# Loading the staged feed-forward weights (sequences 17 to 22) from ScalarE's DMA queue instead of the sync engine's

## The chip, the cores and the metric

The kernel runs on one core of one Trainium2 chip. The metric is the device time of one execution in microseconds; the time of a kernel is the median of several executions. Profiles come from one profiled execution each. TensorE (PE) does matmuls and transposes, VectorE (DVE), ScalarE (ACT) and GpSimd (POOL) do elementwise work, and the sync engine (SP) only issues DMAs. ScalarE can issue DMAs too, through a queue of its own; such an issue stands in its instruction stream between its activations.

## The reference

One transformer block on 16 sequences of 256 rows and 256 features, all in float32: self-attention, cross-attention to a context of 192 features, and a gated feed-forward layer.

```
h = _layernorm(x, ln1_g, ln1_b)
x = _attention(h, h, sa_wq, sa_wk, sa_wv, sa_wo, sa_bo) + x
h = _layernorm(x, ln2_g, ln2_b)
x = _attention(h, cond_emb, ca_wq, ca_wk, ca_wv, ca_wo, ca_bo) + x
h = _layernorm(x, ln3_g, ln3_b)
p = h @ ff_w1 + ff_b1
a, gate = (p[..., :D_FF], p[..., D_FF:])
h = a * jax.nn.gelu(gate, approximate=False) @ ff_w2 + ff_b2
return h + x
```

Attention has 16 heads of 64 features. ff_w1 is 256 x 2048, ff_w2 is 1024 x 256.

## The kernel before, in words

Each matmul operand is split into a rounded high part and a low remainder, and products are made of three passes (high by high, high by low, low by high), so that the result keeps float32 accuracy.

The attention work is cut into 256 slots `c`, one for each pair of heads of each sequence: `seq, pair = divmod(c, PAIRS)` with PAIRS = 8. Sequences 0 to 15 are the self-attention, 16 to 31 the cross-attention of the same 16 inputs. The feed-forward layer runs after slot 255. Each engine runs its own loop over the slots, and semaphores tie the loops together: `pe_slot`, `act_slot`, `dve_slot`, `pool_slot`, and for the sync engine the loop over `c` in its block. All of it is software-pipelined by hand, in written order.

What happens to one pair of heads `k`: TensorE projects its queries and keys into the PSUM bank QKB three slots early (`pe_project`, L342). ScalarE copies QKB, rounded, into QKS (`act_copy_qk`, L470), VectorE writes the low part into QKS (`dve_split_qk`, L604) and so frees QKB for the next projection. The sync engine then copies QKS into RX in four DMAs (`copy_ring`, L434 and L436). TensorE reads RX for the scores S (L303, L304). QKS has two buffers, so ScalarE's copy of `k` waits for the RX copies of `k - 2` to have landed. The scores pass a maximum on VectorE (L616), the exponential on ScalarE (L508, PT), transposes on TensorE (L356, PTB), a rounding copy on ScalarE (L529, PH) with its low part on VectorE (L598, PL), the product with the values (L401, PVB), a copy of half of it on ScalarE (L485, ON), the division by the denominators on POOL (L814), and the output projection (L381, WOP).

In every slot the sync engine issues seven DMAs: two that spread denominators (`spread_den`, L1241), one that saves them (`save_den`, L1230) and the four of `copy_ring`. At pair 0 `store_rows` adds one (L1213), and after that `weights(c)` may add some. ScalarE's queue carries the loads of turned rows (`act_load_rows`, L442, two of its four before the exponentials of pair 1 and two at the end of that slot) and of the context (`act_load_ctx`, L460).

STG is one buffer of 128 partitions by 1024 columns for weights on their way from DRAM. The weights of the cross-attention pass through it in sequences 1 to 6, its output weights after those, and those of the feed-forward layer in sequences 17 to 22: at pair 0 the sync engine waits until POOL has read the previous contents and issues two DMAs of 64 partitions, 256 KB each (L1201). POOL then splits a quarter at each of the pairs 2, 5, 6 and 7 (`pool_split_w`, L756 and L758, into WA), and counts each in `s_pw`. Sequences 17 to 20 bring ff_w1 (rows of 4 KB), 21 and 22 bring ff_w2 (rows of 1 KB).

Of the kernel before, what the change touches and what calls it, by code (L numbers as in the profile page):

```python
# [11 lines left out]
P = 128  # L12
B, S, D = 16, 256, 256
# [6 lines left out]
PAIRS = H // 2  # L20
# [5 lines left out]
CH = 1024  # L26
HC = CH // 2
NCH = 6
HALF = PAIRS // 2
HOLD = 8  # L30
QTR = 4
# [46 lines left out]
def block_kernel(nc, x, ctxt, ln1_g, ln1_b, ln2_g, ln2_b, ln3_g, ln3_b, sa_wq, sa_wk, sa_wv, sa_wo,  # L78
                 sa_bo, ca_wq, ca_wk, ca_wv, ca_wo, ca_bo, ff_w1, ff_b1, ff_w2, ff_b2, out):
    ctx = ExitStack()  # L80
    with ctx:
        def sb(name, shape, dt=F32):
            return ctx.enter_context(nc.sbuf_tensor(name, shape, dt))
# [4 lines left out]
        def sem(name):  # L88
            return ctx.enter_context(nc.semaphore(name))
# [19 lines left out]
        STG = sb("STG", [P, CH])  # L109
# [47 lines left out]
        def await_low(e, n):  # L157

            if n in DVE_LOW:
                e.wait_ge(s_wlo, DVE_LOW.index(n) + 1)  # L160
            else:
                e.wait_ge(s_wlp, POOL_LOW.index(n) + 1)
# [11 lines left out]
        d_wst = sem("d_wst")  # L174
# [15 lines left out]
        s_pw = sem("s_pw")  # L190
        s_oh = sem("s_oh")
        s_ow = sem("s_ow")
# [228 lines left out]
        def act_gain_bias(e, n, k):  # L421

            e.wait_ge(a.dve_th, n)
            h = near(n)[:, k * S:(k + 1) * S]
            e.activation(h, h, ACT.Identity, bias=LNG[:, n // B, 1, k:k + 1],
                         scale=LNG[:, n // B, 0, k:k + 1]).then_inc(a.act_hf, 1)
# [18 lines left out]
        def act_load_rows(e, n, *parts):  # L445

            e.wait_ge(d_hs, 16 * n)
            e.wait_ge(a.s_ht, 2 * n)
            if n >= B:
                e.wait_ge(a.pl_ct, 2 * (n - B + 1))  # L450
            load_turned(e, far(n), HS[0, :, :], d_hl, *parts)
# [21 lines left out]
        def act_slot(e, sl):  # L473
            c = sl.c
            seq, pair = divmod(c, PAIRS)
            prepares = c >= 0 and sl.has(PAIRS * (seq + 1))

            if sl.has(c - 3):
                s = c - 3
                sl.wait(e, a.pe_pv, s + 1)  # L480
                sl.wait(e, a.pl_o, s - 1)
                if s == 0:
                    e.wait_ge(s_ow, HALF)
                for i in range(2):
                    last = e.activation(ON[OWN[i], s % 2, :], PVB[OTHER[i], i * S:(i + 1) * S], ACT.Copy)  # L485
                last.then_inc(a.act_lp, 1)

            if prepares:
                if pair == 1 and seq:
                    act_load_rows(e, seq + 1, 0, 1)  # L490
                if pair in (3, 4):
                    act_gain_bias(e, seq + 1, pair - 3)
            if pair in (3, 4, 5) and sl.has(PAIRS * (seq + 2)) and seq + 2 >= B:
                act_load_ctx(e, seq + 2, *((0,), (3,), (6, 7))[pair - 3])

            if 0 < c < DIRECT:
                act_copy_qk(e, c + 2)

            if sl.has(c):
                sl.wait(e, a.pe_t, c - 1)  # L500
                sl.wait(e, a.dve_rc, c - 1)
                if c == 1:
                    await_low(e, 2)
                for i in range(2):
                    sl.wait(e, a.dve_nm, 2 * c + i + 1)
                    for qt in range(TT):
                        j = i * TT + qt
                        last = e.activation(PT[:, c % 2, j * S:(j + 1) * S], S1[:, i, qt * S:(qt + 1) * S],  # L508
                                            ACT.Exp, bias=NM[:, j:j + 1], accum_out=DEN[:, c % 2, j:j + 1])
                    last.then_inc(a.act_exp, 1)  # L510

            if c == 0:
                act_copy_qk(e, 2)
            elif sl.has(c + AHEAD) and not -1 <= c < DIRECT - 1:
                act_copy_qk(e, c + AHEAD)

            if ATT - 8 <= c < ATT - 6:
                load_ffn_rows(e, 0, 4 * (c - ATT + 8) + 1, 4 * (c - ATT + 8) + 3)

            if c == ATT:  # L520
                e.wait_ge(a.pe_t, ATT - 1)
                e.activation(FG[:, 1, 0:1], B1[:, PAIRS:PAIRS + 1], ACT.Gelu).then_inc(s_tab, 1)
                act_ffn(e, Slot(0, FU, 2))

            if sl.has(c - 1):
                s = c - 1
                sl.wait(e, a.pe_t, s + 1)
                sl.wait(e, a.pe_pv, s - 1)
                e.activation(PH[:, s % 2, :], PTB[:, :, :].rearrange("p i n -> p (i n)"), ACT.Copy) \  # L529
                    .then_inc(a.act_ph, 1)  # L530

            if c in (ATT - 4, ATT - 3):
                act_ffn_h(e, 0, c - ATT + 4)

            if prepares and pair == 1:
                act_load_rows(e, seq + 1, *(range(2, 4) if seq else range(4)))
            if pair in (3, 4) and sl.has(PAIRS * (seq + 2)) and seq + 2 >= B:
                act_load_ctx(e, seq + 2, *((1, 2), (4, 5))[pair - 3])
# [562 lines left out]
        def dve_weights(e, *ns):  # L1101

            for n in ns:
# [6 lines left out]
                else:  # L1110
                    e.tensor_tensor(low, raw(n), hi, ALU.subtract).then_inc(s_wlo, 1)

        def act_attention_slot(e, sl):
            act_slot(e, sl)
            if -AHEAD <= sl.c < 3:
                act_weights(e, *((4,), (5,), (6, 7), (8,), (9, 10), (11,))[sl.c + AHEAD])
            if sl.c == PAIRS * 2:
                e.wait_ge(d_sm, 16 * 5)
# [53 lines left out]
        def _(e):  # L1172
# [24 lines left out]
            def stage(src, dst=STG[:, :]):  # L1197

                h = P // 2
                for part, rows in ((slice(0, h), src[0]), (slice(h, P), src[1])):  # L1200
                    e.dma_start(dst[part], rows).then_inc(d_wst, 16)  # L1201

            def stage_rows(w):

                v = w.rearrange("(g p) n -> p g n", p=P)
                stage((v[0:P // 2], v[P // 2:P]), STG[:, :].rearrange("p (g n) -> p g n", n=D))
# [16 lines left out]
            half = DA // 2  # L1223
# [28 lines left out]
                else:  # L1252
                    stage((w[P:DC, :], w[P:DC, :]))

            def stage_ffn(n):

                if n < 4:
                    w = ff_w1[n // 2 * P:(n // 2 + 1) * P, n % 2 * CH:(n % 2 + 1) * CH]
                    stage((w[0:P // 2, :], w[P // 2:P, :]))
                else:  # L1260
                    stage_rows(ff_w2[(n - 4) * half:(n - 3) * half, :])

            def spill(c):

                seq, pair = divmod(c, PAIRS)
# [11 lines left out]
            def weights(c):  # L1277

                seq, pair = divmod(c, PAIRS)
                if c == 1:  # L1280
                    e.dma_start(BOUT[:, :], sa_bo.partition_broadcast(P)).then_inc(d_bo, 16)
                if 2 <= c < HOLD:
                    await_low(e, c + 4)
                    load_x(xv, c)
                if c == 3:
                    await_low(e, 4)
                    await_low(e, 5)
                    stage_rows(sa_wo[half:, :])
                if c == PAIRS + 2:
                    load_gains(1, ln2_g, ln2_b)  # L1290
                if c == PAIRS + 3:
                    load_gains(2, ln3_g, ln3_b)
                if c == PAIRS + 4:
                    e.dma_start(B1[:, :], ff_b1.rearrange("(k p) -> p k", p=P),
                                allow_slow_non_contiguous=True).then_inc(d_sm, 16)
                if pair == 0 and 1 <= seq <= NCH:
                    if seq == 1:
                        e.wait_ge(s_ow, PAIRS)
                    else:
                        e.wait_ge(s_pw, QTR * (seq - 1))  # L1300
                    stage_cross(seq - 1)
                if c == PAIRS * (NCH + 1) + 1:
                    e.wait_ge(s_pw, QTR * NCH)
                    stage_rows(ca_wo[0:half, :])
                if c == SLOTS - PAIRS - 1:
                    e.wait_ge(a.pl_xb, B)
                    e.dma_start(BOUT[:, :], ca_bo.partition_broadcast(P)).then_inc(d_bo, 16)
                if c == SLOTS + 1:
                    e.wait_ge(s_ow, PAIRS + HALF)
                    stage_rows(ca_wo[half:, :])  # L1310
                if pair == 0 and B + 1 <= seq <= B + NCH:
                    if seq == B + 1:
                        e.wait_ge(s_ow, 2 * PAIRS)
                    else:
                        e.wait_ge(s_pw, QTR * (NCH + seq - B - 1))
                    stage_ffn(seq - B - 1)
                if c == ATT - PAIRS:
                    e.wait_ge(a.pl_xb, 2 * B)
                    e.dma_start(BOUT[:, :], ff_b2.partition_broadcast(P)).then_inc(d_bo, 16)
# [136 lines left out]
```

## Time and profile before

| | |
|---|---|
| median of 3 runs | 1713.91 us |
| lowest to highest | 1712.26 to 1714.52 us |
| profiled execution, its time | 1712.7 us |
| profiled execution, span of the trace | 1710.7 us |
| TensorE busy | 1699.1 us, 99% of the span |
| VectorE busy | 1468.2 us, 86% |
| ScalarE busy | 1186.5 us, 69% |
| GpSimd busy | 1087.7 us, 64% |
| granted TensorE clock | 1.000 |

Issues of DMAs are not counted as busy time. The shares are averages over the whole span, of which the attention slots take the first four fifths. Names such as SPq and ACTq stand for an engine's DMA issues; the duration beside one is that of the issue, not of the transfer.

### The profile page before, as it was taken

To read this page: it belongs to the slowest core of one execution; us is meant where nothing else is said; L and a number is where in the kernel's file an instruction comes from. 1 tells how busy PE (TensorE), PEld (TensorE's weight loads), DVE (VectorE), ACT (ScalarE), POOL (GpSimd) and SP (SyncE) were. 2 spreads that over 40 slices of the span, in tenths; PEclk is the share of its full clock that TensorE was granted. 3 is DMA by queue.
4 is the path that set the end of the run, shared out by engine and by line. 5 is a ranking of instruction groups with operands and counts; after the bars stand their busy time and mean duration, and the time that the engine had idled before them with its cause. 6 is when DMAs were issued, how large, how long until landed. Compare 5 with 4: busy or idle time off the path is not lost.

```text
span 1710.7 us, 42980 instructions
## 1 busy us (share of the span) xinstructions
PE 1699.1 (99%) x13628; PEld 1661.8 (97%) x13628; DVE 1468.2 (86%) x3184; ACT 1186.5 (69%) x3246; POOL 1087.7 (64%) x1812
## 2 busy tenths in 40 slices
PE   8999999999999999999999999999999999999999
PEld 8999999999999999999999999999999998888888
DVE  8888988888888888899999999999999998666665
ACT  7777777777777777777777777887787776222222
POOL 6777777766666666687777887777777666122211
PEclk9999999999999999999999999999999999999999
DMA  7777777676666566667777787776666663212110
GB/s 210 186 187 177 185 182 180 167 181 165 154 156 155 150 161 160 166 166 185 191 189 194 188 194 180 182 181 168 169 170 168 164 167 80 68 50 68 64 42 25
DMA packets 286640, 263.99 MB, mean 154 GB/s; under 512 B 102224, under 2 KB 246736, under 8 KB 286416
## 3 DMA queue, kind: packets, MB, share of 16 engines
q1 hardware_dynamic: 232624, 248.12, 57.2%
q10 hardware_dynamic: 53792, 13.12, 3.7%
q8 instruction: 111, 1.82, 0.4%
q14 instruction: 113, 0.93, 0.2%
HBM read 70.40 MB, written 24.90 MB: 56 GB/s over the span
## 4 chain that ended last, share of the span: by engine, by line
PE 94%; SPq 1%; POOL 1%; DMA 1%; DVE 1%; issue 1%; ACT 1%; ACTq 0%; POOLq 0%; DVEq 0%
PE QKB L342 19%; PE PVB L401 14%; PE PTB L356 12%; PE WOP L381 10%; PE VB L317 9%; PE S L304 7%; PE S L303 7%; PE PTB L923 5%; PE S L923 5%; PE QKB L939 3%; PE VB L939 3%; SPq L434 0%; SPq L436 0%; ACT PT L508 0%; DMA STG<-in_L_xattn_ca_wo_dram 0%
## 5 line engine op out<-in xcount | busy, mean ns | idle before, releaser
L508 ACT ACTIVATE PT<-S,NM 128x256 f32<-128x256 f32 x1024 | 472.1, 474 | 183.9 <-DVE NM L616 183.4
L598 DVE TENSOR_TENSOR PL<-PTB,PH 128x512 fp32r<-128x512 f32 x512 | 349.6, 684 | 80.1 <-ACT PH L529 76.1
L814 POOL TENSOR_TENSOR ON<-ON,RB 128x256 f32<-128x256 f32 x256 | 188.8, 738 | 275.0 <-DVE ON L636 261.6
L616 DVE TENSOR_REDUCE NM<-S 128x2 f32<-128x512 f32 x512 | 326.1, 678 | 0.0
L529 ACT ACTIVATE PH<-PTB 128x1024 fp32r<-128x1024 f32 x256 | 263.5, 1029 | 88.9 <-PE PTB L356 85.8
L356 PE MATMUL PTB<-IDN,PT 128*128 128x128 f32 x2048 | 265.9, 273 | 0.1
L303 PE MATMUL S<-RX 128*128 128x256 f32 x1012 | 253.8, 283 | 0.0
L304 PE MATMUL S<-RX 128*128 128x256 f32 x1012 | 253.7, 283 | 0.0
L356 PEld LDWEIGHTS PTB<-IDN,PT 128*128 128x128 f32 x2048 | 229.5, 140 | 0.9 <-DVE PL L598 0.8
L381 PE MATMUL WOP<-WO,OT 128*128 128x256 f32 x1536 | 226.3, 283 | 1.7 <-POOL OT L819 1.7
L636 DVE TENSOR_TENSOR ON<-PVB,ON 64x256 f32<-64x256 f32 x512 | 213.3, 417 | 3.5
L508 ACT ACTIVATION_READ_ACCUMULATOR PT<-S,NM 128x1 f32 x1024 | 207.9, 203 | 0.0
L485 ACT ACTIVATE ON<-PVB 64x256 f32<-64x256 f32 x512 | 194.3, 379 | 17.4 <-issue 3.0
L381 PEld LDWEIGHTS WOP<-WO,OT 128*128 128x128 f32 x1536 | 202.7, 192 | 2.3 <-POOL OT L819 2.1
L342 PE MATMUL QKB<-HT,WA 128*128 128x256 f32 x1512 | 202.4, 283 | 2.3 <-DVE QKS L604 1.3
L819 POOL TENSOR_TENSOR OT<-ON,OT 128x256 fp32r<-128x256 f32 x256 | 189.7, 741 | 20.5
L795 POOL TENSOR_TENSOR VR<-VF,VR 128x256 fp32r<-128x256 f32 x256 | 189.7, 741 | 20.5
L304 PEld LDWEIGHTS S<-RX 128*128 128x128 f32 x1012 | 194.3, 192 | 0.0
L342 PEld LDWEIGHTS QKB<-HT,WA 128*128 128x128 f32 x1512 | 190.4, 192 | 3.2 <-issue 2.3
L303 PEld LDWEIGHTS S<-RX 128*128 128x128 f32 x1012 | 193.4, 191 | 0.0
L401 PE MATMUL PVB<-PH,VR 128*128 128x256 f32 x1024 | 183.5, 300 | 1.6 <-issue 1.5
L604 DVE TENSOR_TENSOR QKS<-QKB,QKS 128x512 fp32r<-128x512 f32 x254 | 166.0, 654 | 17.0 <-ACT QKS L470 16.9
(143 smaller groups left out, 3140.0 us busy)
## 6 DMA issues: line engine op xcount, KB each, us to landing
RX<-QKS SPq DMA_DIRECT2D x506, 192.0 KB, 2.9
RX<-QKS SPq DMA_DIRECT2D x506, 128.0 KB, 2.8
RB<-denominators SPq DMA_DIRECT2D x512, 64.0 KB, 2.7
out_dram<-XR SPq DMA_DIRECT2D x32, 256.0 KB, 2.7
rows<-XN SPq DMA_DIRECT2D x24, 256.0 KB, 2.4
rows<-HF SPq DMA_DIRECT2D x23, 256.0 KB, 2.6
XR<-in_x_dram SPq DMA_DIRECT2D x16, 256.0 KB, 3.2
denominators<-RDT SPq DMA_DIRECT2D x256, 16.0 KB
```

The lines of the kernel that those rows point to most:

```text
L303: e.matmul(o, q, RX[:, c % 2, i, K1, :], start=True, stop=False)
L304: last = e.matmul(o, q, RX[:, c % 2, i, K2, :], start=False, stop=True)
L342: last = e.matmul(qk_bank(k)[:, m * S:(m + 1) * S], w[:, p * P:(p + 1) * P], act, start=j == 0, stop=j == len(passes) - 1)
L356: last = e.transpose(PTB[:, i, kt * S + qt * P:kt * S + (qt + 1) * P], PT[:, s % 2, q0:q0 + P], IDN[:, :])
L381: last = e.matmul(WOP[:, t * D:(t + 1) * D], OT[:, op, t * P:(t + 1) * P], WO[:, p, wp, :], start=p == 0 and t == 0 and j == 0, stop=p == ...
L401: last = e.matmul(PVB[:, i * S:(i + 1) * S], VR[:, s // 2 % 2, kt, s % 2, i * P:(i + 1) * P], part[:, first:first + S], start=i == 0 and j ...
L485: last = e.activation(ON[OWN[i], s % 2, :], PVB[OTHER[i], i * S:(i + 1) * S], ACT.Copy)
L508: last = e.activation(PT[:, c % 2, j * S:(j + 1) * S], S1[:, i, qt * S:(qt + 1) * S], ACT.Exp, bias=NM[:, j:j + 1], accum_out=DEN[:, c % 2 ...
L529: e.activation(PH[:, s % 2, :], PTB[:, :, :].rearrange("p i n -> p (i n)"), ACT.Copy) \
L598: e.tensor_tensor(PL[:, cols], PTB[:, i, :], PH[:, s % 2, cols].bitcast(F32), ALU.subtract).then_inc(a.dve_pl, 1)
L616: e.tensor_reduce(NM[:, i * TT:(i + 1) * TT], S1[:, i, :].rearrange("p (t s) -> p t s", t=TT), AX.X, ALU.max, negate=True).then_inc(a.dve_ ...
L636: last = e.tensor_tensor(on, PVB[OWN[i], i * S:(i + 1) * S], on, ALU.add)
```

## The change

`stage_ffn` moves from the sync engine's `weights(c)` to `act_attention_slot`. ScalarE now makes the same waits and issues the same twelve DMAs, two at the end of its slot at pair 0 of sequences 17 to 22, behind its PH copy. The destinations, sizes and the semaphore `d_wst`, for which POOL waits, stay.

```diff
         def act_attention_slot(e, sl):
             act_slot(e, sl)
+            seq, pair = divmod(sl.c, PAIRS)
+            if pair == 0 and B + 1 <= seq <= B + NCH:
+                if seq == B + 1:
+                    e.wait_ge(s_ow, 2 * PAIRS)
+                else:
+                    e.wait_ge(s_pw, QTR * (NCH + seq - B - 1))
+                stage_ffn(e, seq - B - 1)
...
+        def stage_ffn(e, n):
+
+            h = P // 2
+            if n < 4:
+                w = ff_w1[n // 2 * P:(n // 2 + 1) * P, n % 2 * CH:(n % 2 + 1) * CH]
+                for rows in (slice(0, h), slice(h, P)):
+                    e.dma_start(STG[rows, :], w[rows, :]).then_inc(d_wst, 16)
+            else:
+                w = ff_w2[(n - 4) * HC:(n - 3) * HC, :].rearrange("(g p) n -> p g n", p=P)
+                to = STG[:, :].rearrange("p (g n) -> p g n", n=D)
+                for rows in (slice(0, h), slice(h, P)):
+                    e.dma_start(to[rows], w[rows]).then_inc(d_wst, 16)
...
-                if pair == 0 and B + 1 <= seq <= B + NCH:
-                    if seq == B + 1:
-                        e.wait_ge(s_ow, 2 * PAIRS)
-                    else:
-                        e.wait_ge(s_pw, QTR * (NCH + seq - B - 1))
-                    stage_ffn(seq - B - 1)
```

ScalarE's stream before, from the end of slot 144 (pair 0 of sequence 18) into slot 145; PT is the exponential, QKS the copy of the projections, PH the rounded transposes, ON the copy of the attention product, HF<-rows the first two row loads of pair 1:

```order
L470 ACTIVATE QKS<-QKB 128x512 [waits d_dup1,pe_qk]
L529 ACTIVATE PH<-PTB 128x1024 [waits pe_pv,pe_t]
L485 ACTIVATE ON<-PVB 64x256 [waits pl_o,pe_pv]
L485 ACTIVATE ON<-PVB 64x256
L442 DMA HF<-rows 32x4x128 [waits pl_ct,s_ht,d_hs]
L442 DMA HF<-rows 32x4x128
L508 ACTIVATE PT,DEN<-S,NM 128x256 [waits dve_nm,dve_rc,pe_t]
```

The same place in the changed kernel:

```order
L470 ACTIVATE QKS<-QKB 128x512 [waits d_dup1,pe_qk]
L529 ACTIVATE PH<-PTB 128x1024 [waits pe_pv,pe_t]
L1119 DMA STG<-in_L_xattn_ff_w_dram 64x1024 [waits s_pw]
L1119 DMA STG<-in_L_xattn_ff_w_dram 64x1024
L485 ACTIVATE ON<-PVB 64x256 [waits pl_o,pe_pv]
L485 ACTIVATE ON<-PVB 64x256
L442 DMA HF<-rows 32x4x128 [waits pl_ct,s_ht,d_hs]
L442 DMA HF<-rows 32x4x128
L508 ACTIVATE PT,DEN<-S,NM 128x256 [waits dve_nm,dve_rc,pe_t]
```

Two DMA issues with a wait for POOL now stand between PH and ON, ahead of the row loads in the same queue.

The sync engine's stream before, at pair 0 of sequence 17 (slot 136) and into slot 137; RX<-QKS are the four ring copies, RB<-denominators and denominators<-RDT the denominators:

```order
L1230 DMA denominators<-RDT 4x32x32 [waits d_rb1,dve_rt]
L434 DMA RX<-QKS 64x768 [waits pe_s,dve_lo]
L436 DMA RX<-QKS 64x2x256
L434 DMA RX<-QKS 64x768
L436 DMA RX<-QKS 64x2x256
L1201 DMA STG<-in_L_xattn_ff_w_dram 64x1024 [waits s_ow]
L1201 DMA STG<-in_L_xattn_ff_w_dram 64x1024
L1241 DMA RB<-denominators 64x256 [waits pl_or,d_ds3]
L1241 DMA RB<-denominators 64x256
L1230 DMA denominators<-RDT 4x32x32 [waits d_rb0,dve_rt]
L434 DMA RX<-QKS 64x768 [waits pe_s,dve_lo]
```

The same place in the changed kernel (L1250 and L1261 are the former L1230 and L1241):

```order
L1250 DMA denominators<-RDT 4x32x32 [waits d_rb1,dve_rt]
L434 DMA RX<-QKS 64x768 [waits pe_s,dve_lo]
L436 DMA RX<-QKS 64x2x256
L434 DMA RX<-QKS 64x768
L436 DMA RX<-QKS 64x2x256
L1261 DMA RB<-denominators 64x256 [waits pl_or,d_ds3]
L1261 DMA RB<-denominators 64x256
L1250 DMA denominators<-RDT 4x32x32 [waits d_rb0,dve_rt]
L434 DMA RX<-QKS 64x768 [waits pe_s,dve_lo]
```

The two loads of STG are gone from between the ring copies of one slot and the denominators of the next; nothing else moved on this engine.

## Rows read from the trace of the kernel before

**Rows 1.** The page: busy time, share of the span, instructions.
```profile
PE 1699.1 (99%) x13628; PEld 1661.8 (97%) x13628; DVE 1468.2 (86%) x3184; ACT 1186.5 (69%) x3246; POOL 1087.7 (64%) x1812
```

**Rows 2.** Timeline, TensorE (start, duration): projections, slot 136, 137, then sequences' starts.
```profile
783.10 0.76 PE L342 MATMUL QKB<-CT,WB 128*128 128x256 f32 x5
...
788.91 0.76 PE L342 MATMUL QKB<-CT,WB 128*128 128x256 f32 x5
...
826.89 0.76 PE L342 MATMUL QKB<-CT,WB 128*128 128x256 f32 x5
...
870.89 0.76 PE L342 MATMUL QKB<-CT,WB 128*128 128x256 f32 x5
...
914.91 0.76 PE L342 MATMUL QKB<-CT,WB 128*128 128x256 f32 x5
...
958.72 0.76 PE L342 MATMUL QKB<-CT,WB 128*128 128x256 f32 x5
...
1002.08 0.76 PE L342 MATMUL QKB<-CT,WB 128*128 128x256 f32 x5
...
1045.64 0.76 PE L342 MATMUL QKB<-CT,WB 128*128 128x256 f32 x5
...
1089.00 0.76 PE L342 MATMUL QKB<-CT,WB 128*128 128x256 f32 x5
```

**Rows 3.** Timeline, TensorE: the projections of slots 154 to 156 (sequence 19).
```profile
881.73 0.82 PE L342 MATMUL QKB<-CT,WB 128*128 128x256 f32 x5
...
887.45 0.86 PE L342 MATMUL QKB<-CT,WB 128*128 128x256 f32 x5
...
893.24 0.76 PE L342 MATMUL QKB<-CT,WB 128*128 128x256 f32 x5
```

**Rows 4.** Timeline, ScalarE and its queue, 873 to 887 us.
```profile
874.61 1.02 ACT L529 ACTIVATE PH<-PTB 128x1024 fp32r<-128x1024 f32 x1
...
875.66 0.38 ACT L485 ACTIVATE ON<-PVB 64x256 f32<-64x256 f32 x1
876.04 1.33 ACTq L442 DMA_DIRECT2D XN<-rows  x1
...
877.49 0.48 ACT L508 ACTIVATE PT<-S,NM 128x256 f32<-128x256 f32 x1 [1.07 <-DVE NM L616]
...
880.31 0.60 ACT L470 ACTIVATE QKS<-QKB 128x512 fp32r<-128x512 f32 x1 [0.88 <-DMA RX<-QKS]
...
886.07 0.60 ACT L470 ACTIVATE QKS<-QKB 128x512 fp32r<-128x512 f32 x1 [0.87 <-DMA RX<-QKS]
```

**Rows 5.** Timeline, the sync engine's issues, same stretch.
```profile
875.49 0.62 SPq L436 DMA_DIRECT2D RX<-QKS  x1
876.14 1.87 SPq L1201 DMA_DIRECT2D STG<-in_L_xattn_ff_w_dram  x2
878.12 1.18 SPq L1241 DMA_DIRECT2D RB<-denominators  x2
...
880.09 0.49 SPq L434 DMA_DIRECT2D RX<-QKS  x1
...
881.96 0.62 SPq L436 DMA_DIRECT2D RX<-QKS  x1
```

**Rows 6.** Timeline, VectorE: the low part of QKS for pair 155.
```profile
874.82 0.65 DVE L604 TENSOR_TENSOR QKS<-QKB,QKS 128x512 fp32r<-128x512 f32 x1
```

**Rows 7.** Timeline, POOL: the last quarter read from STG before slot 152.
```profile
869.18 0.75 POOL L758 TENSOR_TENSOR WA<-STG,WA 128x256 fp32r<-128x256 f32 x1
```

**Rows 8.** The DMAs issued from 780 to 1010 us: KB each, median us to landing.
```profile
RX<-QKS SPq DMA_DIRECT2D x83, 192.0 KB, 2.9
...
STG<-in_L_xattn_ff_w_dram SPq DMA_DIRECT2D x12, 256.0 KB, 4.9
```

**Rows 9.** Waits of ScalarE from 780 to 1010 us: total, times, longest.
```profile
ACT QKS L470 <- DMA RX<-QKS: 7.7, 8, 1.4
```

**Rows 10.** Window of sequence 23: length, busy PE, PEld, DVE, ACT, POOL, clock, DMA, GB/s.
```profile
1045.64:1089.00 43.36, 43.36 (x370) 43.36 (x369) 40.73 (x90) 34.71 (x99) 32.10 (x56) 1.00 0.75 187
```

More of the change, by code:

```diff
@@ L1253, in stage_cross @@
                     stage((w[P:DC, :], w[P:DC, :]))
[L1255 to L1259, printed above, removed]
-                else:
-                    stage_rows(ff_w2[(n - 4) * half:(n - 3) * half, :])
             def spill(c):
@@ L1310, in weights @@
                     stage_rows(ca_wo[half:, :])
-                if pair == 0 and B + 1 <= seq <= B + NCH:
-                    if seq == B + 1:
-                        e.wait_ge(s_ow, 2 * PAIRS)
-                    else:
-                        e.wait_ge(s_pw, QTR * (NCH + seq - B - 1))
-                    stage_ffn(seq - B - 1)
                 if c == ATT - PAIRS:
```

## The prediction

> **What bounds the kernel now.** I read the page first, then TensorE's timeline slot by slot, then the same stretch on the other engines. TensorE is busy for 1699.1 of 1710.7 us [rows 1], so all its gaps together are 11.6 us, and no change of queues can bring more. What the moved loads can have to do with any of it is read from the starts of TensorE's projections at pair 0 [rows 2]. Sequence 23, without staging, takes 1089.00 - 1045.64 = 43.36 us, or 5.42 a slot. The six sequences with staging take 43.79, 44.00, 44.02, 43.81, 43.36 and 43.56, which is 0.43, 0.64, 0.66, 0.45, 0.00 and 0.20 more: 2.38 us together. Of the first 0.43, 0.39 belongs to slot 136 itself (788.91 - 783.10 = 5.81), before a byte of ff_w1 has been asked for. So about 2.0 us of the span stand beside the staging at all, nearly all of it in sequences 18 to 20.
>
> How the 0.66 of sequence 19 comes about is in its rows. In slot 154 and 155 TensorE loses 5.72 - 5.42 = 0.30 and 5.79 - 5.42 = 0.37 [rows 3]. ScalarE's copy of QKS began at 880.31 and again at 886.07, both after waiting some 0.9 us for an RX copy to land [rows 4], and a late QKS makes the VectorE split late, which frees QKB for the next projection. The second of these waits is for the ring copies issued from 880.09 to 882.58. Their source was ready at 874.82 + 0.65 = 875.47 [rows 6], so they went out 4.6 us late, because the sync engine issues in order and was busy: the two loads of STG took it 1.87 us, then denominators, then the copies [rows 5]. VectorE has no room to catch up: it is busy for 40.73 of 43.36 us even without staging [rows 10]. ScalarE met such a wait 8 times in this stretch, 7.7 us in all, the longest 1.4 [rows 9].
>
> **The change, part by part.** *Removed from the sync engine:* two issues a sequence. In sequence 19 the sync engine was free at 875.49 + 0.62 = 876.11 and began the denominators of the next slot at 878.12 [rows 5]; without the loads that is 2.0 us sooner, and so are the copies behind them: 878.1 to 880.6 in place of 880.09 to 882.58. The last is issued at 879.95 in place of 881.96; with the 2.9 us from issue to landing [rows 8] it lands near 882.9, and even with the 4.1 that it took here (881.96 to 886.07) at 884.1, 2.0 us ahead of 886.07, so the second wait goes. The first (880.31) is for ring copies issued before the loads and is not helped by this. Sequence 21 shows no loss at all with the same staging on the same queue [rows 2], so a staging as such need not cost anything; I take it that the losses of 18, 19, 20 and 22 go with the second wait: 0.64 + 0.66 + 0.45 + 0.20 = 1.95 us. The lower bound is nothing, if another late thing stands right behind.
>
> *Added to ScalarE:* twelve issues. An issue does not occupy its arithmetic, but what is behind it in the stream waits. Nothing shows this DMA on ACTq, so I bound it: the pair is 1.87 us here on the sync engine as the dear end [rows 5], and 0.6 each, 1.2 us, by the ring copy's row (875.49, 0.62) of the same order of size as the cheap end. The issues can begin when PH has been handed to the engine at 874.61 [rows 4], so they end between 875.8 and 876.5, where ON now starts at 875.66; ON moves by 0.2 to 0.8 us. The two row loads of pair 1 come next; the second took 1.33 us beside the two STG issues of the sync engine, and it is its end (877.37) that let the exponentials go at 877.49 [rows 4]. With the sync engine's STG issues gone it should be nearer to the ring copy's 0.6. So the exponentials of slot 153 start between 877.1 and 878.3, against 877.49 now: 0.4 sooner to 0.8 later. Behind them stands the QKS copy, which waits until 880.31 anyway: the exponentials now end at about 879.4, 0.9 before it, which covers the 0.8. If the cover were gone, TensorE would lose about what it lost in slot 154, 0.30. I take half of that, 0.15 for each of six sequences, 0.9 us.
>
> The new wait costs nothing: POOL finished the last quarter at 869.18 + 0.75 = 869.93 [rows 7], 4.7 us before ScalarE comes to it. POOL's own need is distant: it reads STG two slots later, and the landing of 4.9 us [rows 8] starts about 1.5 us earlier than now. ScalarE's row loads now stand behind 512 KB in their queue, but only the last two of the four, a slot later, decide when the rows are there.
>
> *The transfers themselves:* same bytes. They begin at about 874.7 in place of 876.14, from another queue than the ring copies of the same slot (873.6 to 876.1). This is what speaks against the change. Where rows show it: the ring copies of that slot, issued before the loads, landed just ahead of 880.31, 4.8 us after the last of them was issued at 875.49, where the median is 2.9 [rows 4, 5, 8]; the loads disturb even copies that were issued before them, by 1.9 us. 512 KB at the 187 GB/s of this stretch [rows 10] is 2.8 us of the engines' time. From below the added delay is nothing (they are disturbed already), from above the whole 2.8 us, if all of the loads is served ahead of them. I take a value near nothing, because the loads will be 1.4 us further on when the last ring copy is issued.
>
> The Trainium skill, page "DMA: Bandwidth & Descriptors", sections "Queues, rings and completion order" and "Issuing engines are not separate DMA queues", says that each DMA engine takes turns between the queues that have work, a packet at a time, and that issuing from several engines only saves the sequencer's issue time. By that rule the ring copies lose the place ahead of the loads that they have in one queue, and what is saved is the sync engine's 1.87 us alone; it makes the rival of the shared turns below more likely than the rows alone would, and leaves the sum as it is.
>
> Sum: -1.95 + 0.9 = -1.05 us. The profiled execution was 1712.7 us, a span of 1710.7 and 2.0 around it; it would be 1711.65, with a span of 1709.65. The median of the runs is 1713.91, 1.2 above the profiled one, so I predict 1712.9. A measurement of this kernel can tell about 0.2%, 3.4 us, from no change; the runs before spread over 2.3 us.
>
> **The rivals.**
> *Nothing moves* (25%). The second wait goes, but the losses have another cause, such as VectorE's row turn in the same slot, or ScalarE gives all of it back. For it: sequence 17 loses 0.39 in slot 136 with no staging near it [rows 2], so such losses have other sources. Time 1713.9, plus or minus 0.4.
> *All is won* (12%). ScalarE's issues are wholly hidden: -1.95, a time of 1712.0.
> *The ring copies of the same slot give way to the loads* (15%), the case on the other side. The loads take their turns on the DMA engines between ring copies that until now were ahead of them. The first wait grows by up to 2.8 us; QKS, split and projection follow, as VectorE has no room. It decides once the landing is late by more than about 0.3 us beyond now, since at 880.31 the split only just meets the projection at 881.73 [rows 3]. Price: at half of it, 1.4 - 0.3 = 1.1 us in each of six sequences, 6.6, less the 1.95 won: +4.65, 1718.6; at a quarter, 0.7 - 0.3 = 0.4 each, 2.4 less 1.95, +0.45, 1714.4. Against it: the copies have 1.4 us less of loads ahead of their end than behind them now.
> *ScalarE's issues get long* (8%). If each of the two takes the 1.33 of the row load that was issued beside others [rows 4], the pair ends at 877.3, the row loads 1.7 us later, and exponentials start at 879.0, 1.5 late; 0.9 is covered, 0.6 is not: 3.6 over six, less 1.95, +1.6, 1715.6.
>
> The Trainium skill, page "Perfetto Trace Analysis", section "DMA Instruction — HWDGE (DVE, Sync)", says that the two issuing engines share one descriptor generator, and that the profiled time of an issue holds the wait for its lock. The 1.33 us row load beside the 1.87 us pair agrees with it [rows 4, 5].
>
> **How the numbers follow.** The forecast (1712.4 to 1713.4 by its own terms) has 40%, the rivals 25, 12, 15 and 8. The gain cannot pass 2.4 us, and a change of over 3.4 us down needs something outside this stretch: faster 0.03. Over 3.4 us up needs the half of the ring rival's chance that lies at such delays: 0.08. Same: 0.89. The range goes from 1711.2 (all is won, and the spread of a median of three) to 1715.8 (the cheap part of the ring rival, and the long issues).
>
> **What would show it.** In the changed profile: sequences 18 to 20 at 43.4 to 43.6 us between projections, against 44.0; no wait of QKS for RX in slot 154, 162 and so on, one left in the slot before; ring copies at pair 1 issued some 2 us sooner; the STG issues on ACTq at 0.6 to 0.95 us each, beginning within PH; the exponentials of the next slot within 0.8 us of the 5.42 us beat. I would be wrong if the wait of pair 1's QKS copy grows beyond 1.4 us, or if these sequences get longer than 44.0.

## The result and the profile after

The changed kernel takes 1717.08 us (median of 17 executions) against 1713.32 for the kernel before (17 executions), a ratio of 1.0022 with a 95% interval of 1.0016 to 1.0029. It is slower by 3.8 us. Predicted were 1712.9 us, a small gain, with a range of 1711.2 to 1715.8. One of these executions took 4702.53 us, and one of e3_sp_early below 2049.97; both were disturbed, and the ratios leave them out. The profiled execution took 1719.83 us, one of the longer ones, with a span of 1717.9; what its profile loses is therefore more than the 3.8 us between the medians.

The page of the changed kernel, its busy times and the chain that ended last:

```profile
PE 1700.6 (99%) x13628; PEld 1662.6 (97%) x13628; DVE 1467.7 (85%) x3184; ACT 1185.0 (69%) x3246; POOL 1085.2 (63%) x1812
...
PE 87%; POOL 3%; SPq 2%; DMA 2%; ACT 2%; DVE 2%; issue 2%; POOLq 0%; ACTq 0%; DVEq 0%
```

The instructions are as many as in [rows 1]. Only TensorE is busy longer, by 1.5 us (its weight loads by 0.8), and the span is 7.2 us longer: the other 5.7 us are waiting. Where it is can be read from windows that end at TensorE's projection at pair 0 of each sequence, here sequences 18 to 23 (length, busy PE, PEld, DVE, ACT, POOL, granted clock, DMA, GB/s):

```profile
826.93:872.48 45.55, 43.89 (x370) 43.48 (x369) 40.66 (x90) 34.55 (x99) 34.60 (x61) 1.00 0.76 183
872.48:917.64 45.16, 43.85 (x370) 43.44 (x369) 40.63 (x90) 34.53 (x99) 34.57 (x61) 1.00 0.77 185
917.64:961.00 43.36, 43.36 (x370) 43.36 (x369) 40.75 (x90) 34.67 (x99) 34.79 (x61) 1.00 0.80 192
961.00:1008.20 47.20, 45.27 (x370) 44.86 (x369) 40.76 (x90) 34.66 (x99) 34.77 (x61) 0.96 0.75 177
1008.20:1052.64 44.44, 44.05 (x370) 43.50 (x369) 40.56 (x90) 34.48 (x99) 34.53 (x61) 1.00 0.78 187
1052.64:1096.00 43.36, 43.36 (x370) 43.36 (x369) 40.71 (x90) 34.65 (x99) 31.97 (x56) 1.00 0.76 188
```

Sequence 23, without staging, takes 43.36 us as before. In excess of that, sequences 18, 19, 21 and 22 take 2.19, 1.80, 3.84 and 1.08 us; sequence 20 takes none, and sequence 17 (783.02 to 826.93, not shown) 0.55. The six make 9.46 us, against 2.38 before [rows 2]. That difference, 7.1 us, is the whole difference of the two spans.

The waits of the changed kernel from 780 to 1045 us say what for (total, times, longest):

```profile
ACT QKS L470 <- DMA RX<-QKS: 10.0, 5, 3.5
PEld S L303 <- DMA RX<-QKS: 5.3, 4, 1.9
PE S L303 <- DMA RX<-QKS: 4.5, 4, 1.7
```

TensorE now waits for RX itself, four times; in the whole profile before it never did. Sequence 18 shows how. ScalarE and its queue at the end of slot 144 and in slot 145:

```profile
830.65 1.03 ACT L529 ACTIVATE PH<-PTB 128x1024 fp32r<-128x1024 f32 x1
830.65 1.15 ACTq L1119 DMA_DIRECT2D STG<-in_L_xattn_ff_w_dram  x2
831.91 0.38 ACT L485 ACTIVATE ON<-PVB 64x256 f32<-64x256 f32 x1 [0.23 <-issue]
832.04 1.37 ACTq L442 DMA_DIRECT2D HF<-rows  x1
...
834.20 0.48 ACT L508 ACTIVATE PT<-S,NM 128x256 f32<-128x256 f32 x1 [1.52 <-DVE NM L616]
...
838.49 0.60 ACT L470 ACTIVATE QKS<-QKB 128x512 fp32r<-128x512 f32 x1 [2.35 <-DMA RX<-QKS]
```

The two loads of STG are issued beside the PH copy, and hold ON up by 0.23 us. The next exponentials start 7.27 us behind the projection of pair 0, against 6.33 before, but it is the QKS copy that stands still, for 2.35 us, until the ring copies of slot 144 have landed. The same landing, at 838.45, is what TensorE's scores wait for; when they are done, the next projection still waits 0.20 us for the split of that late QKS copy:

```profile
838.45 0.39 PE L303 MATMUL S<-RX 128*128 128x256 f32 x1 [1.47 <-DMA RX<-QKS]
...
839.86 0.86 PE L342 MATMUL QKB<-CT,WB 128*128 128x256 f32 x5 [0.20 <-DVE QKS L604]
```

These are the sync engine's issues at the same time:

```profile
829.23 0.75 SPq L434 DMA_DIRECT2D RX<-QKS  x1
830.03 0.62 SPq L436 DMA_DIRECT2D RX<-QKS  x1
830.71 0.60 SPq L434 DMA_DIRECT2D RX<-QKS  x1
831.35 2.07 SPq L436 DMA_DIRECT2D RX<-QKS  x1
833.52 1.19 SPq L1261 DMA_DIRECT2D RB<-denominators  x2
```

The loads of STG (830.65 to 831.80) fall between the second and the fourth ring copy. The two L436 copies of this slot, minimum, median and maximum from issue to landing:

```profile
DMA to landing us min/median/max: 4.6/5.8/7.1
```

In the kernel before, the same two of sequence 18 took

```profile
DMA to landing us min/median/max: 3.5/4.2/5.0
```

and in sequence 21, before, 2.8 to 3.1. The last ring copy takes 2.1 us longer to land than before, and 3.2 us longer in sequence 21, where it is 6.3 in place of 3.1. Two other things add to the lateness. In sequence 18 the issue of that copy alone took 2.07 us in place of 0.62, beside a row load on ScalarE's queue (832.04); it isn't needed for the damage, since in sequence 19 this issue took 0.62 us and the copy still landed after 6.6 us in place of 4.7. In sequence 21 the ring copies were issued 1.0 us later than before, behind a row store (L1233, the former L1213) whose issue took 1.63 us in place of 0.53.

What TensorE loses follows from the point at which the last ring copy of pair 0 lands. In sequences 18 to 22 of the changed kernel that is 11.5, 11.1, 8.6, 11.7 and 10.2 us behind the projection of pair 0, and the slot of pair 1 takes 2.08, 1.72, 0.00, 2.36 and 0.81 us more than 5.42: each about the time by which the landing passes 9.4 us. Before, it landed at 9.6, 9.3, 8.9, 7.5 and 7.7 us, and the slot of pair 1 lost 0.19 us in sequence 18 and nothing in the others. So the copies of sequences 18 and 19 had no slack left before the change.

In sequence 21 something is added. After the stall, TensorE's granted clock fell (changed kernel, windows of 2 us):

```profile
970.00:972.00 2.00, 1.04 (x9) 0.84 (x8) 0.00 (x0) 0.00 (x0) 1.77 (x4) 1.00 1.13 211
972.00:974.00 2.00, 1.22 (x8) 1.02 (x8) 0.55 (x1) 1.18 (x2) 1.45 (x3) 0.98 1.12 255
974.00:976.00 2.00, 1.80 (x8) 1.80 (x9) 1.78 (x4) 1.32 (x4) 0.00 (x0) 0.50 1.09 218
976.00:978.00 2.00, 2.00 (x14) 2.00 (x13) 1.82 (x5) 2.00 (x9) 0.31 (x1) 0.67 0.78 172
978.00:980.00 2.00, 2.00 (x19) 2.00 (x19) 1.79 (x5) 0.82 (x2) 1.76 (x4) 1.00 0.78 199
```

TensorE was half idle for four microseconds, then ran at 0.50 of full speed, the 1.2 GHz level, for 2 us and was back at 2.4 GHz within the next two. The slot after the stall took 6.88 us between projections in place of 5.42, so the clock took up to 1.5 us of this profile. The 2 us windows around the stall in sequence 18 (834 to 844 us) all have clock 1.00; sequence 21 has the longer of the two stalls.

### The profile page after: what moved, and what is told of

Its sections match the earlier page's. It is cut to its first block, busy times and chain, and to the rows that moved or that the text cites. A ratio compares the mean times of both kernels' runs of the same rounds, so it can differ in the third digit from the quotient of the medians.

```text
span 1717.9 us, 42980 instructions
## 1 busy us (share of the span) xinstructions
PE 1700.6 (99%) x13628; PEld 1662.6 (97%) x13628; DVE 1467.7 (85%) x3184; ACT 1185.0 (69%) x3246; POOL 1085.2 (63%) x1812
## 4 chain that ended last, share of the span: by engine, by line
PE 87%; POOL 3%; SPq 2%; DMA 2%; ACT 2%; DVE 2%; issue 2%; POOLq 0%; ACTq 0%; DVEq 0%
PE QKB L342 18%; PE PVB L401 12%; PE PTB L356 11%; PE WOP L381 9%; PE VB L317 8%; PE S L304 6%; PE S L303 6%; PE PTB L923 5%; PE S L923 5%; PE QKB L939 3%; PE VB L939 3%; DMA RX<-QKS 1%; ACT PT L508 1%; SPq L434 1%; ACT PH L529 1%
```

## The experiments

Three theories. BYTES: the 512 KB of a staging share the DMA engines with the ring copies of pair 0, which are short of time, and now start among them rather than behind them. STREAM: the two issues hold up ScalarE's own work. QUEUE: a second queue by itself, taking turns with the sync engine's, delays the ring copies, whenever the loads start. The kernel before was measured beside each of them; its median was 1713.48 us beside e1 to e4, 1713.88 beside e5 to e8 and 1713.42 beside e9 to e11.

### e1_act_tiny: the changed kernel with a quarter of each load

```diff
-                    e.dma_start(STG[rows, :], w[rows, :]).then_inc(d_wst, 16)
+                    e.dma_start(STG[rows, 0:QW], w[rows, 0:QW]).then_inc(d_wst, 16)
...
-                    e.dma_start(to[rows], w[rows]).then_inc(d_wst, 16)
+                    e.dma_start(to[rows, 0:1], w[rows, 0:1]).then_inc(d_wst, 16)
```

> The twelve loads stay where the change put them on ScalarE, but bring a quarter of the columns (64 KB each in place of 256 KB), so that the feed-forward weights and the output are not the real ones. Theory BYTES (the loads now start about 1.5 us sooner, among the ring copies of the same slot, and share the DMA engines with them): the ring copies land in time, the waits of TensorE for RX are gone, and the kernel is 1 to 2 us below the kernel before (about 1712). Theory STREAM (the two issues hold up ScalarE's exponentials and copies): the issues are as many and as long, so the time stays near that of the changed kernel, 3 to 4 us above the kernel before.

Measured: 1711.81 us, ratio 0.9992 (0.9983 to 1.0001), 1.7 us below the kernel before, as BYTES has it. Sequences 18 to 21 in its windows:

```profile
828.94:872.30 43.36, 43.36 (x371) 43.36 (x369) 40.63 (x90) 34.53 (x99) 34.65 (x61) 1.00 0.74 183
872.30:915.66 43.36, 43.36 (x371) 43.36 (x369) 40.62 (x90) 34.67 (x99) 34.71 (x61) 1.00 0.75 183
915.66:959.02 43.36, 43.36 (x371) 43.36 (x369) 40.74 (x90) 34.65 (x99) 34.79 (x61) 1.00 0.73 183
959.02:1002.38 43.36, 43.36 (x371) 43.36 (x369) 40.63 (x90) 34.70 (x99) 34.79 (x61) 1.00 0.74 183
```

TensorE never waits in them, with all twelve issues in ScalarE's stream. In one place the issues were even long, and the exponentials waited for them (ScalarE, sequence 18):

```profile
832.66 2.41 ACTq L1119 DMA_DIRECT2D STG<-in_L_xattn_ff_w_dram  x2
835.16 0.38 ACT L485 ACTIVATE ON<-PVB 64x256 f32<-64x256 f32 x1 [1.48 <-POOL OT L819]
...
836.31 0.47 ACT L508 ACTIVATE PT<-S,NM 128x256 f32<-128x256 f32 x1 [0.38 <-issue]
```

and that sequence is 43.36 us long like the others. STREAM falls as the cause of the changed kernel's loss. (For ff_w1 the quarter is rows of 1 KB in place of 4, of the same number. Whether what counts is the bytes or the length of the rows this run doesn't separate; e6_act_split below moves whole rows away instead.)

### e2_sp_tiny: the kernel before with a quarter of each load

```diff
-                    stage((w[0:P // 2, :], w[P // 2:P, :]))
+                    stage((w[0:P // 2, 0:QW], w[P // 2:P, 0:QW]), STG[:, 0:QW])
...
-                    stage_rows(ff_w2[(n - 4) * half:(n - 3) * half, :])
+                    w = ff_w2[(n - 4) * half:(n - 3) * half, :].rearrange("(g p) n -> p g n", p=P)
+                    stage((w[0:P // 2, 0], w[P // 2:P, 0]), STG[:, 0:QW])
```

> The loads are on the sync engine as before, a quarter of the columns each, so the output is not the real one. It shows what the bytes of the staging cost in the kernel before. BYTES: 1 to 2 us below the kernel before, near e1_act_tiny. If the sync engine's lateness by the issues were what costs the kernel before its 2 us, as the prediction had it, the time stays at the kernel before and e1_act_tiny is faster than this by 1 to 2 us. STREAM says that e1_act_tiny is slower than this by 3 to 5 us.

Measured: 1711.98 us, ratio 0.9991 (0.9982 to 1.0000), the same as e1_act_tiny. So the bytes of the staging cost the kernel before most of its 2 us, and the sync engine's issues little. The profiles leave the issues something: the six sequences exceed 43.36 by 1.22 us here and by 0.58 in e1_act_tiny, 0.39 and 0.40 of these in sequence 17. The times don't resolve that 0.6. ScalarE still waits for RX 8 times here, 4.9 us in all from 780 to 1045 us, and never in e1_act_tiny: the issues do make ring copies late, and TensorE feels little of it.

### e3_sp_early and e11_sp_early_look: the sync engine's queue, right ahead of the ring copies

```diff
+                seq, pair = divmod(c, PAIRS)
+                if pair == 0 and B + 1 <= seq <= B + NCH:
...
+                    stage_ffn(seq - B - 1)
                 if 0 <= c - 1 + AHEAD < ATT and c - 1 >= -AHEAD:
                     k = c - 1 + AHEAD
```

(The same lines are taken out of `weights(c)`, as in e10_sp_first. e11_sp_early_look is the same kernel again, with a profile to read.)

> The full loads on the sync engine's queue, ahead of the four ring copies of the same slot in place of behind them. BYTES, in the form that the start ahead of the ring copies is what counts, whichever the queue: ring copies land 2 us or more later than before, TensorE waits for RX in most of the six sequences, 4 to 12 us above the kernel before. Theory QUEUE (a second queue taking turns is what delays the ring copies, not when the loads start): only the 1.3 us of later issue counts, 0 to 2 us above the kernel before.

> The kernel of e3_sp_early once more, for its profile. BYTES: TensorE waits for RX in most of the sequences 17 to 22, and the last of the four ring copies of pair 0 takes 5 to 7 us from issue to landing, against 3.1 to 5.0 in the kernel before.

Measured: 1721.16 us, ratio 1.0040 (1.0027 to 1.0054), and 1722.28 for the single execution of e11_sp_early_look. With one queue only, the loss is twice that of the changed kernel. The waits of e11_sp_early_look from 780 to 1045 us:

```profile
ACT QKS L470 <- DMA RX<-QKS: 15.2, 6, 3.6
PEld S L303 <- DMA RX<-QKS: 6.1, 5, 1.8
PE S L303 <- DMA RX<-QKS: 5.0, 4, 1.6
```

In its sequence 19 the L436 copies took 4.6 to 5.4 us to land, and they were issued 1.1 to 1.2 us later than before as well. Of the 1.9 us by which the last one landed later, 1.2 are the later issue and 0.7 the transfer, so this run alone doesn't separate the two; e10_sp_first does. The loss of 7.7 us is far above the 0 to 2 that QUEUE allowed, so a second queue is not needed for the damage: QUEUE falls as the cause, BYTES stands.

### e4_act_pair1: ScalarE's queue, behind the first row loads of pair 1

```diff
                     act_load_rows(e, seq + 1, 0, 1)
+                if pair == 1 and B + 1 <= seq <= B + NCH:
...
+                    stage_ffn(e, seq - B - 1)
```

(In e4, e5 and e7 the lines of the change are taken out of `act_attention_slot`.)

> The full loads on ScalarE's queue, but behind the first two row loads of pair 1, about 2 us later than in the changed kernel and near the time at which the sync engine issued them. BYTES: within 1 us of the kernel before, or up to 1.5 us faster since the sync engine is free. QUEUE: still 3 to 4 us slower, since the queue is the second one. STREAM: 3 us or more slower, since the exponentials of pair 1 now stand right behind the issues.

Measured: 1714.16 us, ratio 1.0003 (0.9994 to 1.0012). On the second queue, but near the old time, the loads cost what they cost before. TensorE never waited for RX. This is the other half of the answer on QUEUE. The gain from a freed sync engine did not show either. On STREAM the answer is less clean: the issues stood right ahead of the exponentials, and in sequence 20, where the row loads ahead of them were late too, these waited 3 us:

```profile
923.96 0.47 ACT L514 ACTIVATE PT<-S,NM 128x256 f32<-128x256 f32 x1 [2.99 <-issue]
```

That sequence took 1.88 us more than 43.36, with its last ring copy landed 7.5 us behind the projection, in good time. So in this place ScalarE's stream can cost TensorE something; the median doesn't resolve it. POOL waited 5 times for STG, 6.4 us in all, which TensorE's waits don't show.

### e5_act_on: ScalarE's queue, 4.5 us earlier than the change put them

```diff
                 last.then_inc(a.act_lp, 1)

+            if pair == 0 and B + 1 <= seq <= B + NCH:
...
+                stage_ffn(e, seq - B - 1)
```

> The full loads on ScalarE's queue at the same pair 0, but ahead of the exponentials, 4 us earlier than in the changed kernel, so that the 2.8 us of transfer are mostly over when the sync engine issues the ring copies of this slot. BYTES, if what counts is the overlap with those four ring copies and their small slack: the waits of TensorE for RX are gone, and the kernel is 0.5 to 2 us below the kernel before. If what counts is any start ahead of the ring copies (as a simple reading of e3_sp_early has it): 4 us or more above. The ring copies of the slot before have about 1 us more slack and take the disturbance.

Measured: 1712.71 us against 1713.88, ratio 0.9990 (0.9981 to 0.9998): faster than both kernels, if only just. The loads, on ScalarE's queue, and the ring copies of the same slot, on the sync engine's, in sequence 19:

```profile
871.59 0.48 ACTq L1125 DMA_DIRECT2D STG<-in_L_xattn_ff_w_dram  x1
...
872.11 0.62 ACTq L1125 DMA_DIRECT2D STG<-in_L_xattn_ff_w_dram  x1
```

```profile
875.00 0.63 SPq L434 DMA_DIRECT2D RX<-QKS  x1
...
876.99 0.62 SPq L436 DMA_DIRECT2D RX<-QKS  x1
```

The L436 copies land in 3.3 to 4.0 us, and what is left of ScalarE's waits for RX from 780 to 1045 us is

```profile
ACT QKS L470 <- DMA RX<-QKS: 0.7, 2, 0.4
```

against 8.7 us before in the same stretch and 10.0 after the change. Sequences 18 to 20 take 43.36 us each. So it is not any start ahead of the ring copies that hurts; 3.4 us ahead is harmless, and 0.3 to 1.4 us behind the first of them is the bad place (in sequence 20 not even that).

### e6_act_split: one load at pair 0, one at pair 1

```diff
-                stage_ffn(e, seq - B - 1)
+                stage_ffn(e, seq - B - 1, slice(0, P // 2))
...
                     act_load_rows(e, seq + 1, 0, 1)
+                    if B + 1 <= seq <= B + NCH:
+                        stage_ffn(e, seq - B - 1, slice(P // 2, P))
```

> The first load stays where the change put it, the second goes behind the first two row loads of pair 1. BYTES: half of the burst among the ring copies, so their landing is late by about half (1 us in place of 2 to 3.5), which the slack nearly covers: 0 to 1.5 us above the kernel before. A theory by which the mere order of issue counts: 3 us above.

Measured: 1714.43 us against 1713.88, ratio 1.0000 (0.9992 to 1.0009). Half of the burst in the bad place costs nothing that can be told by the time. In its profile TensorE waited twice for RX, 1.5 us, against four times and 4.5 us in the changed kernel, and the slots of pair 1 lost 1.26 us in sequence 18 and 1.44 in sequence 20, whose last ring copies landed at 10.6 and 10.8 us.

### e7_act_pair1_exp: ScalarE's queue, behind the exponentials of pair 1

```diff
+            if pair == 1 and B + 1 <= seq <= B + NCH:
...
+                stage_ffn(e, seq - B - 1)
             if c == 0:
                 act_copy_qk(e, 2)
```

> The full loads on ScalarE's queue behind the exponentials of pair 1, 4 to 5 us later than in the changed kernel. BYTES: the ring copies of pair 0 are out of reach, those of pair 1 share with the loads, in the slot where the sync engine is not held up by a row store: 0.5 us above to 1.5 us below the kernel before, if POOL, which wants STG at pair 2, is not kept waiting for more than 2 us. If POOL's wait for STG decides, POOL's waits for this DMA appear in its list and it is 1 to 4 us above.

Measured: 1717.45 us against 1713.88, ratio 1.0016 (1.0007 to 1.0025). Its waits from 780 to 1045 us have both:

```profile
ACT QKS L470 <- DMA RX<-QKS: 10.6, 7, 2.7
POOL WA L762 <- DMA STG<-in_L_xattn_ff_w_dram: 10.6, 6, 2.4
```

The ring copies of pair 1 are hit now, and POOL waits for STG every time. The expectation, that pair 1's copies have room for it, was wrong. TensorE's own waits in the same stretch name the ring copies' side and never POOL:

```profile
PE S L303 <- DMA RX<-QKS: 0.8, 1, 0.8
PE QKB L342 <- DVE QKS L610: 0.6, 3, 0.2
```

The slot of pair 2 loses 1.37, 0.53, 0.67, 0.20 and 0.15 us in sequences 18 to 22, and that of pair 3 some 0.35 in each. What holds up pair 3 no row names.

### e8_sp_pair1: the sync engine, one slot later

```diff
-                if pair == 0 and B + 1 <= seq <= B + NCH:
+                if pair == 1 and B + 1 <= seq <= B + NCH:
```

> The full loads on the sync engine as before, one slot later, behind the ring copies of pair 1. BYTES with the sync engine's issues counted (0.2 to 0.5 us by e2_sp_tiny): within 1 us of the kernel before unless POOL waits for STG; then 1 to 6 us above, with the wait in POOL's list.

Measured: 1715.34 us against 1713.88, ratio 1.0006 (0.9997 to 1.0015): 1.5 us, at the edge of what can be told. POOL's wait is there, and it is much longer than in e7_act_pair1_exp:

```profile
POOL WA L756 <- DMA STG<-in_L_xattn_ff_w_dram: 24.0, 6, 4.7
```

TensorE now does wait for POOL, for a small part of that:

```profile
PE WOP L381 <- POOL OT L819: 2.5, 4, 1.0
```

24.0 us of waiting on POOL cost the median 1.5 us, so e7's 10.6 us of the same wait, without such an entry for TensorE, are unlikely to be its 3.6 us. That points to its ring copies: ScalarE waited 10.6 us for RX there and 3.4 us here.

### e9_act_half: the changed kernel with half of each load

```diff
-                    e.dma_start(STG[rows, :], w[rows, :]).then_inc(d_wst, 16)
+                    e.dma_start(STG[rows, 0:HC], w[rows, 0:HC]).then_inc(d_wst, 16)
```

(The ff_w2 loads are halved too, by `0:2` of their four parts.)

> The changed kernel with half of the columns in each load (128 KB each), so the output is not the real one: the same issues at the same place, half of the bytes. BYTES: the landing of the ring copies of pair 0 is late by about half of what it is in the changed kernel, which the slack of 2 us mostly covers: between e1_act_tiny and the changed kernel and nearer to the former, 1.5 us below to 1 us above the kernel before. If the number of loads rather than their bytes counted: 3 to 4 us above.

Measured: 1713.47 us against 1713.42, ratio 0.9999 (0.9990 to 1.0008). With e1_act_tiny and the changed kernel this makes a series: with the same issues at the same place, 128, 256 and 512 KB a sequence give -1.7, 0.0 and +3.8 us. In the profile of the middle one the last ring copies of sequences 18, 19 and 21 land at 9.9, 9.8 and 9.7 us, and the slots of pair 1 lose 0.53, 0.49 and 0.34: just beyond the same 9.4.

### e10_sp_first: the sync engine's queue, 5 us earlier than the kernel before

```diff
             for c in range(-AHEAD, ATT + 2):
+                seq, pair = divmod(c, PAIRS)
+                if pair == 0 and B + 1 <= seq <= B + NCH:
...
+                    stage_ffn(seq - B - 1)
                 if c >= 2:
                     spread_den(c - 2)
```

> The full loads on the sync engine at the very start of its slot at pair 0, ahead of the denominators, 3 us before the ring copies rather than right before them. BYTES: the transfers are mostly over when the ring copies are issued, but these go out 1.3 us later for the two issues on the same engine: 0 to 2 us above the kernel before, far below e3_sp_early. If any start ahead of the ring copies on the same queue delays them by the whole transfer: as e3_sp_early, 6 us or more above.

Measured: 1711.77 us against 1713.42, ratio 0.9990 (0.9980 to 0.9999). It is as good as e5_act_on, on the old queue. The price of 0 to 2 us for later ring copies that was expected does not show in the time. The profile has it once: in sequence 19 the last ring copy was issued 2.0 us later than before and landed at 10.2 us, and the slot of pair 1 lost 0.78. The sync engine's issues in its sequence 19:

```profile
870.77 1.35 SPq L1201 DMA_DIRECT2D STG<-in_L_xattn_ff_w_dram  x2
872.22 2.34 SPq L1241 DMA_DIRECT2D RB<-denominators  x2
...
875.96 0.51 SPq L434 DMA_DIRECT2D RX<-QKS  x1
```

The loads are issued 5.2 us ahead of the ring copies, of which the L436 land in 2.8 to 3.5 us. The same queue with the same order of loads and ring copies gives 1721.2 (e3_sp_early) or 1711.8, by where in the slot the loads are. Late issue is not the difference: the last ring copy of pair 0 is issued 5.8 to 6.7 us behind the projection here and 5.4 to 6.8 in e11_sp_early_look (sequences 18 to 22). Its way from issue to landing is, 3.1 to 3.5 us here and 4.5 to 5.7 there.

## Why the prediction was wrong

The step that failed is the one on the transfers themselves: "I take a value near nothing, because the loads will be 1.4 us further on when the last ring copy is issued." It was bounded by 0 and 2.8 us, and the added delay of the last ring copy is 2.1 us in sequence 18, 1.9 in 19, 3.2 in 21 and 2.5 in 22. That is near the far bound and beyond it; only sequence 20 has none. (The bound took 187 GB/s from a stretch in which the DMA engines were busy 0.75 of the time [rows 10]; that is what was moved in it, not what the engines can move.) That the loads begin sooner does not put them out of the way sooner: loads and ring copies are in flight together. Before, the four copies of sequence 18 took 3.0, 3.5, 3.6 and 5.0 us, so that mainly the last was disturbed; now they take 2.8, 4.6, 5.9 and 7.1, all from the second on.

The rival of the ring copies, which had 15%, is what happened, by the path that it gave: the first wait grows, and QKS, split and projection follow. It left out that TensorE's scores wait for the same landing, and the slack that it took, 0.3 us, was more than the 0.1 that the landing at 9.3 us in sequence 19 had before the 9.4. Its price was about right. It took 1.1 us a sequence at half of the 2.8 us, before the 1.95 us won, and a time of 1718.6. Against the medians, 3.8 + 1.95 is 5.7 us, 1.0 a sequence; in the long profiled execution (9.46 - 2.38 + 1.95) / 6 is 1.5, of which 0.2 is the clock.

*What bounds the kernel* was right in its place and in part wrong in its reason. The 2 us that stand beside the staging are there, and e1, e2, e5 and e10 get some 1.2 to 1.7 us of them. But the prediction gave them to the sync engine's issues, through the second wait. e2_sp_tiny keeps these issues, drops three quarters of the bytes, and is as fast as e1_act_tiny. By the profiles the bytes have the larger part (2.38 - 1.22 = 1.2 us) and the issues the smaller (1.22 - 0.58 = 0.6).

*Removed from the sync engine*: the second wait did go. In sequence 18 of the changed kernel the wait of 838.49 is the only one of that sequence, and the slot of pair 3, which lost 0.36, 0.37 and 0.37 us in sequences 18 to 20 before, loses nothing. This part of the gain was won, and drowned. That the issues alone caused it is not shown: e4_act_pair1, with the issues off the sync engine and all of the bytes, still loses 0.28, 0.28 and 0.36 in these slots, and e2_sp_tiny, the other way round, 0.37, 0.23 and 0.00.

*Added to ScalarE*: bounded by 1.2 and 1.87 us a pair of issues, measured 1.15 to 1.6 in the changed kernel (2.41 once in e1_act_tiny); ON moves by 0.23 (here) to 0.49 us. The row loads behind them did not get short, as was expected: the first took 1.37 us in sequence 18. So the exponentials start 0.94 us later there, a little beyond the 0.8 of the prediction. That cover hides it was right all the same, and the 0.9 us taken for it was too much: e1_act_tiny shows nothing, with exponentials later still. As an explanation of this kernel, the rival of long issues is out too.

*The new wait and POOL*: nothing, as predicted. POOL has no entry for STG of the feed-forward weights in the changed kernel's list from 780 to 1045 us.

The Trainium skill's rule from "DMA: Bandwidth & Descriptors", "Queues, rings and completion order", that a DMA engine takes turns between queues, pointed to the right rival. The runs don't show that the turns are the reason: the changed kernel on two queues and e3_sp_early on one both delay the ring copies, and e4_act_pair1 on two queues leaves TensorE no wait for them. What it says beside that, that issuing from another engine only saves the sequencer's issue time ("Issuing engines are not separate DMA queues"), agrees: e5_act_on and e10_sp_first, on two queues and on one, both have the ratio 0.9990.

Open is why sequence 20 is spared in the changed kernel's profile, and sequence 17 nearly so. In both 18 and 20 the loads are issued 1.4 us behind the first ring copy (830.65 against 829.23, 921.36 against 919.94), yet the L436 copies take up to 7.1 us in one and 4.4 in the other. So the offset of the issues alone does not decide it. Sequence 20 is spared in the profile of e9_act_half too (43.36 us, beside 43.98 and 43.94 in 18 and 19), but not in that of e6_act_split. The changed kernel's executions spread from 1714.0 to 1721.6, against 1710.6 to 1714.5 before; whether another set of sequences is hit in each of them no run here tests. Open is also what the loads and the ring copies share, the DMA engines or the memories behind them: the runs vary bytes and time, and nothing else.

## What to carry to other kernels

A prefetch that nobody waits for can still set the time, through the bytes that it puts among small transfers that somebody does wait for. Before moving one, find out when the latency-critical transfers land and when they are needed. Here the last ring copy of pair 0 was needed 9.4 us behind the projection and landed at 9.3 and 9.6 us in two of the six sequences, so nearly all of any further delay was a loss. Put the burst well ahead of them (3.4 and 5.2 us were enough here), or make it smaller; which queue it goes through was worth nothing that could be measured. And count who waits for a DMA by name: a wait for RX that begins with the staging in flight is evidence on the bytes first, and on the issuing queue second.

## What the runs showed of the hardware

A pair of 256 KB loads raised the landing of a 128 KB SBUF copy from about 3 us to 4.7 or 5.0 when issued right behind it (kernel before, sequences 18 and 19), to 4.5 to 5.7 when issued right ahead of its group of four on the same queue (e11_sp_early_look), and to 5.7 to 7.1 in four of six sequences when issued among the group from the other queue (changed kernel, sequences 18, 19, 21 and 22). Issued 3.4 us ahead (e5_act_on) or 5.2 us ahead (e10_sp_first) they left it at 3.5 to 4.6 and 3.1 to 3.5 us. Two issues of a DMA of 64 rows of 4 KB cost ScalarE's stream 1.15 us in sequence 18, nearly all of it beside an activation of 1.03 us that was already handed over. And a stall of TensorE brought on by this can cost twice: after the longest one the granted clock was 0.50 for 2 us.
